# Top-54 memory attention: the cut of the scores moves from a VectorE mask after the exponential to two GpSimd passes before it

## The reference, cut to what matters

```python
def _L0_xattn_ref(x, W_qkv, W_o, beta_q, beta_k, gate, log_tau, K_mem, V_mem, clip_k):   # clip_k = 54
    Q = (x @ W_qkv.T)[..., :D]
    coef = (alpha * beta_q + (1.0 - alpha) * beta_k) * D ** -0.5 * tau
    scores = coef * jnp.einsum('bsd,bnd->bsn', Q, K_mem)          # (4, 256, 1601)
    scores = scores - jnp.max(scores, axis=-1, keepdims=True)
    thr = jax.lax.top_k(scores, clip_k)[0][..., -1:]
    scores = jnp.where(scores < thr, -jnp.inf, scores)
    att = jax.nn.softmax(scores, axis=-1)
    return jnp.einsum('bsn,bnd->bsd', att, V_mem) @ W_o.T
```

## Time and profile before

| what | value |
|---|---|
| median of three runs | 3806.7 us |
| the profiled execution: its time, its span | 3805.95 us, 3804.2 us |
| busy over the span: PE, DVE, ACT, POOL | 3511.9, 2341.9, 2242.7, 857.9 us |
| first stage: runs from 0 to about | 274 us |
| busy in the first stage: PE, DVE, ACT, POOL | 187.16, 230.13, 80.83, 4.05 us |

### The profile page before, as it was taken

One profiled execution on the slowest core, in us unless ns is written; L12 is line 12 of the kernel. 1 busy time (PEld: TensorE's weight loads), 2 busy tenths in 40 slices (PEclk: granted clock), 3 DMA queues, 4 the chain that ended last, 5 costly groups with the idle time before them and its releaser, 6 DMA issues. The chain is left out here.

```text
span 3804.2 us, 63574 instructions
## 1 busy us (share of the span) xinstructions
PE 3511.9 (92%) x23912; PEld 3004.1 (79%) x23912; DVE 2341.9 (62%) x4207; ACT 2242.7 (59%) x5208; POOL 857.9 (23%) x1078
## 2 busy tenths in 40 slices
PE   7757969999999999998699999888999999999989
PEld 5657957888889888987556665577988989889878
DVE  8876766776676676663677777434555555545434
ACT  3315746676676666665376666415666666666643
POOL 0003124322232222220120220103232322223214
PEclk7778979999999999999799999898999999999989
DMA  5205521010010010000200000111010010100001
GB/s 179 87 0 215 207 96 48 15 55 26 18 49 23 23 52 15 18 12 9 99 1 36 36 1 1 72 55 59 23 55 29 21 52 26 55 23 18 12 24 41
DMA packets 59473, 179.55 MB, mean 47 GB/s; under 512 B 6117, under 2 KB 27809, under 8 KB 54177
## 3 DMA queue, kind: packets, MB, share of 16 engines
q1 hardware_dynamic: 53312, 136.10, 10.5%
q0 software_dynamic: 3696, 37.68, 2.7%
q10 hardware_dynamic: 2160, 1.71, 0.2%
HBM read 147.14 MB, written 24.13 MB: 45 GB/s over the span
## 5 line engine op out<-in xcount | busy, mean ns | idle before, releaser
L1044 PE MATMUL ps<-a_v_rows,a_probs 128*128 128x129 f32 (+1 forms) x7168 | 943.1, 276 | 0.5 <-DVE a_o_rows L1378 0.5
L1044 PEld LDWEIGHTS ps<-a_v_rows,a_probs 128*128 128x128 f32 (+1 forms) x7168 | 894.4, 191 | 41.0 <-issue 5.1
L1127 ACT ACTIVATE a_probs<-ps 128x512 f32<-128x512 f32 (+1 forms) x896 | 535.1, 597 | 607.1 <-PE ps L1033 606.1
L1353 DVE TENSOR_REDUCE a_neg<-ps 128x1 f32<-128x1024 f32 (+2 forms) x512 | 539.7, 1055 | 397.7 <-PE ps L1008 397.1
L1137 ACT ACTIVATE ps<-a_negb 128x512 f32<-128x512 f32 (+1 forms) x892 | 536.7, 602 | 58.0 <-DVE a_negb L1368 30.2
L1196 POOL TENSOR_SCALAR a_diag<-ident,a_negmax 128x128 fp32r<-128x128 f32 x256 | 156.8, 612 | 1466.9 <-DVE a_negmax L1361 1465.2
L1029 PE MATMUL ps<-a_qt,a_kt 128*128 128x512 f32 (+1 forms) x896 | 427.9, 478 | 1.6 <-PEq L72 1.6
L935 PE MATMUL ps<-a_wr,a_ct 128*128 128x256 f32 (+1 forms) x2496 | 363.1, 288 | 18.6 <-DMA a_ct<-ctx_lo 16.6
L935 PEld LDWEIGHTS ps<-a_wr,a_ct 128*128 128x128 f32 (+1 forms) x2496 | 336.5, 188 | 44.1 <-issue 15.4
L1033 PE MATMUL ps<-a_qt,a_kt 128*128 128x512 f32 (+1 forms) x896 | 355.2, 396 | 0.0
L1031 PE MATMUL ps<-a_qt,a_kt 128*128 128x512 f32 (+1 forms) x896 | 354.0, 395 | 0.0
(11 more groups left out here) (476 smaller groups left out, 6017.8 us busy)
## 6 DMA issues: line engine op xcount, KB each, us to landing
a_wf<-in_a_wq SPq DMA_DIRECT2D x32, 512.0 KB, 3.6
a_wf<-in_a_wo SPq DMA_DIRECT2D x32, 512.0 KB, 3.6
a_ct<-ctx_hi SPq DMA_DIRECT2D x8, 1090.0 KB, 7.8
a_ct<-ctx_lo SPq DMA_DIRECT2D x8, 1090.0 KB, 10.1
f_we<-in_f_experts SPq DMA_DIRECT2D x8, 1088.0 KB, 8.9
a_wf<-in_a_wkv SPq DMA_DIRECT2D x32, 256.0 KB, 2.7
ctx_hi<-a_ct SPq DMA_DIRECT2D x4, 1602.0 KB, 5.4
ctx_lo<-a_ct SPq DMA_DIRECT2D x4, 1602.0 KB, 8.9
```

Of the source, the lines that this page charges most:

```text
L1044: ins = pe.matmul(m.ps[:, 6 + i // 2, (i % 2) * 256:(i % 2) * 256 + VW], probs[0:r, n % 3, i * P:(i + 1) * P], v_rows[g % 2][0:r, t, :], s ...
L1127: act.activation(probs[0:r, n % 3, :], m.ps[0:r, 4 + n % 2, :], ACT.Exp)\
L1353: ins = dve.tensor_reduce(neg2[:, j, r % 2:r % 2 + 1], flat2(m.ps[:, rough_at(task):rough_at(task) + 2, :])[:, 0:e - a0], AX.X, ALU.max, n ...
```

## The change: what it does

After the seventh round of a tile GpSimd makes a cut copy `kept` of the scores in two passes: (raw < threshold) times -3e38, then plus raw. ScalarE's exponential reads `kept` in place of `raw` and sums the row itself (`accum_out`). VectorE's `mask` goes; the reciprocal stays as `inverse`. There is one `kept` buffer, and `best` has two halves, one for each parity of j. `turn_weights` waits for the exponential in place of the mask. On ScalarE `exp(b, 0)` moves into `items(b+1)`, ahead of the third item from the end. On VectorE `output_low` and `add_output` of tile (b-1, 1) stand one round later, and `output_low(b, 0)` stands behind the whole search of tile (b, 1).

```diff
+    EXP_AT = NI - 3
-        best = st.sb("best", [P, 8])
+        best = st.sb("best", [P, 2, 8])
+        kept = st.sb("kept", [P, CTX])
...
-                    pe.wait_ge(mask_ok, j + 1)
+                    pe.wait_ge(exp_ok, j + 1)
...
-                def items(b):
+                def items(b, exp_of=None):
                     for j, task in enumerate(ITEMS):
+                        if j == EXP_AT and b:
+                            exp(exp_of, 0)
                         high(b, task)
...
                 def exp(b, q):
                     act.wait_ge(neg_ok, j + 1)
+                    act.wait_ge(kept_ok, j + 1)
                     if b:
                         act.wait_ge(pt_turned, (j - QT + 1) * len(PT))
-                    act.activation(expd[:, q, :], raw[b % 2][:, q, :], ACT.Exp, bias=negm[:, q:q + 1]).then_inc(exp_ok, 1)
+                        act.wait_ge(inv_ok, j - QT + 1)
+                    act.activation(expd[:, q, :], kept[:, :], ACT.Exp, bias=negm[:, q:q + 1],
+                                   accum_out=rsum[:, 0, q:q + 1]).then_inc(exp_ok, 1)
...
                 keep(0, 0)
-                exp(0, 0)
                 keep(0, 1)
                 for b in range(B):
-                    if b:
+                    if b + 1 < B:
+                        items(b + 1, b)
+                    else:
                         exp(b, 0)
-                    if b + 1 < B:
-                        items(b + 1)
                     take_weights(b, 0)
                     take_output(b, 0)
                     exp(b, 1)
...
+                def keep_largest(b, q):
+                    j = QT * b + q
+                    pool.wait_ge(top_ok, j + 1)
+                    if j:
+                        pool.wait_ge(exp_ok, j)
+                    step(pool.tensor_scalar(kept[:, :], raw[b % 2][:, q, :], best[:, j % 2, AT:AT + 1], -3.0e38,
+                                            ALU.is_lt, ALU.mult))
+                    pool.tensor_tensor(kept[:, :], kept[:, :], raw[b % 2][:, q, :], ALU.add).then_inc(kept_ok, 1)
...
-                def mask(b, q):
-                    dve.wait_ge(exp_ok, QT * b + q + 1)
-                    step(dve.scalar_tensor_tensor(out=expd[:, q, :], in0=raw[b % 2][:, q, :],
-                                                  scalar=best[:, AT:AT + 1], in1=expd[:, q, :],
-                                                  op0=ALU.is_ge, op1=ALU.mult, accum_out=rsum[:, 0, q:q + 1]))
-                    dve.reciprocal(rsum[:, 1, q:q + 1], rsum[:, 0, q:q + 1]).then_inc(mask_ok, 1)
+                def inverse(b, q):
+                    dve.wait_ge(exp_ok, j + 1)
+                    if b:
+                        dve.wait_ge(y_done, j - QT + 1)
+                    dve.reciprocal(rsum[:, 1, q:q + 1], rsum[:, 0, q:q + 1]).then_inc(inv_ok, 1)
...
-                        if r == 3 and b:
+                        if r == 4 and b:
+                            inverse(b - 1, 1)
                             output_low(b - 1, 1)
-                        if r == 4 and b:
+                        if r == 5 and b:
                             add_output(b - 1, 1)
-                    mask(b, 0)
                     for r in range(ROUNDS):
                         largest(b, 1, r)
-                        if r == 5:
-                            output_low(b, 0)
+                        if r == 3:
+                            inverse(b, 0)
+                    output_low(b, 0)
                     add_output(b, 0)
-                    mask(b, 1)
+                inverse(B - 1, 1)
```

More of the change, by code:

```diff
@@ L214, in memory_attention @@
             st.sem(n) for n in "w_scaled w_hi w_lo kact dstep zeroed coef_ok var_ok rstd_ok z_ok".split()]
-        item_ready, item_hi, item_rest, item_free, s_ready, raw_ok, neg_ok, exp_ok, mask_ok = [
-            st.sem(n) for n in "item_ready item_hi item_rest item_free s_ready raw_ok neg_ok exp_ok mask_ok".split()]
+        item_ready, item_hi, item_rest, item_free, s_ready, raw_ok, neg_ok, exp_ok, top_ok = [
+            st.sem(n) for n in "item_ready item_hi item_rest item_free s_ready raw_ok neg_ok exp_ok top_ok".split()]
+        pstep, kept_ok, inv_ok = [st.sem(n) for n in "pstep kept_ok inv_ok".split()]
         minus_ok, pt_turned, pt_ok, o_ready, o_hi, o_lo, y_ready, y_done = [
@@ L447, in keep @@
                     if b >= 2:
-                        act.wait_ge(mask_ok, j - 2 * QT + 1)
+                        act.wait_ge(kept_ok, j - 2 * QT + 1)
                     act.activation(raw[b % 2][:, q, :], flat2(m.ps[:, 0:4, :])[:, 0:CTX], ACT.Copy).then_inc(raw_ok, 1)
@@ L504, in _, with root @@
                     pool.memset(ct[i][:, :, CTX:CTXP].bitcast(F32), 0.0).then_inc(zeroed, 1)
-                for b in range(B):
+                step = Step(pool, pstep)
+                def keep_largest(b, q):
[6 more added lines that the diff above has]
+                    pool.tensor_tensor(kept[:, :], kept[:, :], raw[b % 2][:, q, :], ALU.add).then_inc(kept_ok, 1)
+                def root(b):
                     pool.wait_ge(var_ok, b + 1)
@@ L508, in _ @@
                                        ALU.pow).then_inc(rstd_ok, 1)
+                root(0)
+                for b in range(B):
+                    if b + 1 < B:
+                        root(b + 1)
+                    for q in range(QT):
+                        keep_largest(b, q)
             @block.vector
@@ L531, in largest @@
                 def largest(b, q, r):
+                    j = QT * b + q
                     left = raw[b % 2][:, q, :] if r == 0 else work[:, :]
+                    eight = best[:, j % 2, :]
                     if r == 0:
-                        dve.wait_ge(raw_ok, QT * b + q + 1)
-                    step(dve.max(out=best[:, :], in_=left))
-                    if r == 0:
[L538 to L543, removed]
-                def mask(b, q):
-                    dve.wait_ge(exp_ok, QT * b + q + 1)
-                    step(dve.scalar_tensor_tensor(out=expd[:, q, :], in0=raw[b % 2][:, q, :],
-                                                  scalar=best[:, AT:AT + 1], in1=expd[:, q, :],
-                                                  op0=ALU.is_ge, op1=ALU.mult, accum_out=rsum[:, 0, q:q + 1]))
-                    dve.reciprocal(rsum[:, 1, q:q + 1], rsum[:, 0, q:q + 1]).then_inc(mask_ok, 1)
+                        dve.wait_ge(raw_ok, j + 1)
+                        if j >= 2:
+                            dve.wait_ge(kept_ok, j - 1)
+                    if r == ROUNDS - 1:
+                        dve.max(out=eight, in_=left).then_inc(top_ok, 1)
+                        return
+                    step(dve.max(out=eight, in_=left))
+                    if r == 0:
+                        if j >= 2:
+                            dve.wait_ge(exp_ok, j - 1)
+                        dve.tensor_scalar(negm[:, q:q + 1], eight[:, 0:1], -1.0, None, ALU.mult).then_inc(neg_ok, 1)
+                    step(dve.match_replace(out=work[:, :], in_to_replace=eight, in_values=left, imm_value=-3.0e38))
+                def inverse(b, q):
+                    j = QT * b + q
+                    dve.wait_ge(exp_ok, j + 1)
+                    if b:
+                        dve.wait_ge(y_done, j - QT + 1)
+                    dve.reciprocal(rsum[:, 1, q:q + 1], rsum[:, 0, q:q + 1]).then_inc(inv_ok, 1)
                 def output_low(b, q):
@@ L560, in add_output @@
                     dve.wait_ge(y_ready, QT * b + q + 1)
+                    dve.wait_ge(inv_ok, QT * b + q + 1)
                     dve.scalar_tensor_tensor(out=m.x[:, QT * b + q, :], in0=m.ps[:, 7, 0:D],
```

## The result

The changed kernel takes 3832.8 us (median of four runs, 3827.4 to 3835.0) against 3807.2 for the kernel before (four runs beside it): ratio 1.0059, 95% interval 1.0047 to 1.0072. It is slower by 0.6%, as forecast in direction, but by 25.6 us, where 10 were forecast; the time lies above the range's upper end of 3829. The profiled execution has a span of 3825.6 us, 21.4 more than before.

What follows compares the result with a forecast made beforehand. VectorE's search was taken to bound the first stage. Masks -16.1, reciprocals +0.7, hidden outputs -3.5, waits -5.4, GpSimd latency with exponential +30.6 and copy +4.5 gave +10.8: 3817 us, range 3810 to 3829.

Steps and rivals of the forecast that it cites:

- The bound and the mechanism: First stage: VectorE's search sets the pace; at batch ends VectorE waits for GpSimd, exponential and copy instead of masking.
- L: Latency of the two GpSimd passes with handovers, from the seventh MAX8 to the exponential: 5.85 us, ends 4.8 and 11.6.
- the first GpSimd pass: The compare-and-multiply pass making the cut copy, 1601 columns: 2.1 us, ends 1.6 and 7.65.
- the sum: All gains and costs of the first stage added: +10.8 us.
- the forecast's own rule: Each microsecond of GpSimd latency costs four, one for each batch end.
- The second pass: GpSimd's sum of two tensors, 1601 columns: 3.6 us, between 3.0 and 3.75.
- The waits in the middle: VectorE's waits for a projection in batches 1 and 2: from 5.78 and 3.23 to 3.1 and 0.55 us, -5.4.
- a lower clock: TensorE idles more at batch ends; at a lower clock the 0.55 us wait is 3.1, the time 3819.5 us.
- Masks and hidden outputs: VectorE: eight masks with reciprocals go, -16.1 us; outputs of tile (b, 0) hide in batch-end waits, -3.5 us.
- the lock: VectorE held while GpSimd passes of tiles (b, 0) run beside its search: four times 5.7 us more, 3840 us.
- the second rival: Longer GpSimd latency (scalar pass costing by the column), or VectorE held during passes: 3821 to 3840 us, chance 0.15.

Runs made afterwards that it cites:

- the multiplication alone: Changed kernel with the first GpSimd pass cut to one operation, a multiplication by the number 1.0, so nothing is cut; 3830.7 us.
- the second profile: Profile of the changed kernel measured once more with nothing edited; 3829.9 us (five runs), ratio 1.0065.

## Why the prediction was wrong, step by step

**The bound and the mechanism** were right: VectorE's search paces the stage, and the wait that takes the mask's place is GpSimd, exponential and copy in a row (at the last batch end without the copy). It appears at four batch ends and nowhere else. The kernel without the first pass showed that L counts four times (5.95 us at each end, 23.7 of the stage), the one with the copy first showed that the queue on ScalarE is what passes it on (15.4 for three ends).

**The step that failed** is the first GpSimd pass, "the fixed part is 0.48 and the pass 1.6 + 0.48 = 2.1. I take that, since the cast is the row nearest in size". It took 5.70, and the sum counts it four times. A cast and a tensor-scalar pass are not one kind of work on this engine: 1.0 ns a column against 2.7 for one operation and 3.5 for two. The row of 612 ns at 128 columns was the right kind. Between it and the one-operation pass with a column (4.34 us at 1601) lie 2.5 ns a column and a fixed part of 0.29, and my split gave its columns 0.13 of 0.61. That is 2.24 of the 3.6 us missed; the other 1.36 is the second operation, which the forecast names and prices at nothing. So L was 9.0 us (77.09 to 86.09) and not 5.85, which by the forecast's own rule adds 4 x 3.15 = 12.6 us to its 10.8: 23.4. The profile of before had what sizes the fixed part, in rows that the forecast doesn't use (line, form, count, busy us, mean ns):

```profile
L1168 POOL TENSOR_SCALAR a_k_sq<-a_k_sq 128x1 f32<-128x1 f32 x16 | 3.1, 191 | 3.0 <-ACT a_v_rows L1094 3.0
L3330 POOL TENSOR_SCALAR a_sq<-a_sq 128x4 f32<-128x4 f32 x8 | 1.6, 196 | 43.5 <-ACT a_square L3234 43.4
```

Tensor-scalar work of 1 and 4 columns takes 0.19 and 0.20 us; most rows of 1 to 8 columns lie between that and 0.28, one is at 0.75. So 0.2 to 0.3 of the 0.61 at 128 columns is fixed, and the rest is 2.8 to 3.4 ns a column, which gives an estimate of 4.7 to 5.6 us at 1601. That its upper end comes so near 5.70 is luck: the row at 128 columns has one operation, for which 4.34 was measured, and the overshoot happens to make up for the second.

The pass did lie between the forecast's two ends, 1.6 and 7.65, but the forecast went by size of tile instead of by kind of operation. The Trainium skill (GPSIMD Engine Reference, 4.1 Engine selection) has one-input work on GpSimd roughly at line rate; the cast in the earlier trace rows agrees with its 1.0 ns a column, no tensor-scalar pass here does. The second pass, forecast at 3.6 of 3.0 to 3.75, took 3.02 at the batch ends.

**The waits in the middle** were put at 3.1 and 0.55 us and were 0 and 1.70 (0 and 0.28 in the second profile). In batch 1 the projection came 24.8 us after the batch's start, not 28.05; the `weighted` ahead of it took 6.07 us, against 7.70 before and in the multiplication alone, where the wait is 1.84. So these waits move with the clock from run to run. The granted clock in 82 to 116 us, of the changed kernel and of the one before:

```profile
82.00:116.00 34.00, 22.09 (x132) 18.20 (x131) 26.77 (x31) 12.35 (x20) 4.63 (x3) 0.85 0.35 110
```
```profile
82.00:116.00 34.00, 26.40 (x135) 22.45 (x134) 27.74 (x30) 12.48 (x22) 0.70 (x1) 0.70 0.16 49
```

The forecast leaned towards a lower clock because TensorE would idle more. In this stretch it was busy for less time and was granted more. That doesn't show that idling raised the clock: busy time times clock is nearly the same in both (18.8 and 18.5), so the shorter busy time is what the higher clock gives by itself. At the end of the stage the last `weighted` took 6.07 us, against 8.63 before, and the part behind the last reciprocal 12.35 in place of 15.1. That part was 14.2 in the second profile, with 1.4 us less of waits, and the stage came out the same, so the two nearly cancel. These two places take 1.9 and 2.75 off the 23.4; 0.17 less at each of three batch ends and small things bring it to the 18.0 measured.

**Masks and hidden outputs**: no mask remains, the search's own instructions kept their 1.81 to 1.83 us beside a GpSimd pass, and the first pass took 5.70 us beside a search and alone, so the lock of the second rival is not there. The outputs at a batch end are hidden, as said. The rule of the Trainium skill (SBUF — State Buffer, Who interferes with whom) that one-input instructions of VectorE don't contend holds here.

**The rivals.** What came is the second rival by its first mechanism, a longer L, given 0.15. It deserved more, since its row was the only one of its kind. The range's upper end was also misread: 3829 takes in a first pass of 5.1 us, which is little more than half the way from 2.1 to 7.65 and not two thirds.

## What to carry to other kernels

Price an operation by the row of its own kind, even if that row is twelve times smaller, and only then by size; take the fixed part from the smallest rows of that kind, and don't take a second operation as free. When work moves off a busy engine, ask at each place what is queued behind whoever now waits for it: here a copy of the next tile stood behind the exponential, and one move in the order was worth 15 of 18 us. Try a new order in the old kernel as well, or its gain is put down to the moved work. Hide the moved work under the next tile, and at the last tile, where there is no next, leave it on the fast engine.

## What the hardware showed that was not expected

- GpSimd tensor-scalar passes of 128x1601 fp32: 4.27 us with one operation, 5.62 with two, 0.08 more with the scalar from a column; comparison, subtraction and multiplication alike. Both are slower than the sum of two tensors of that size, 2.86 to 3.62 us.
- That sum takes 2.86 us with one tensor as both inputs, and 3.02 or about 3.6 with two inputs, by where one of them begins.
- In 82 to 116 us the granted clock was 0.85 in the changed kernel and 0.70 in the one before, though TensorE was forecast to get less of it. No run shows what raised it.
